# Three rotating score banks and one expert bank in the first layer of a two-layer attention kernel

## The chip, the cores and the metric

One Trainium2 chip, one core. The metric is device time in microseconds (us) of one execution; times are medians of several executions, and the profile is of one further execution.

## The reference

For 16 batches of 256 tokens of width 256 the reference applies two layers, each with an attention block and a feed-forward block. In layer 0 the feed-forward block holds a small attention across the 16 heads of each token, followed by eight dense experts weighted by a softmax gate:

```python
x = x + tanh(g_xattn[0]) * L0_xattn(layernorm(x), ctx, ctx, mask, causal)   # 16 heads of 64
x = x + tanh(g_ffn[0])   * L0_ffn(layernorm(x))
x = x + tanh(g_xattn[1]) * L1_xattn(layernorm(x), ctx, ctx)                 # 16 heads of 16
x = x + tanh(g_ffn[1])   * L1_ffn(layernorm(x))

# inside L0_ffn, b tokens, h2 the normalised middle result
att  = softmax(einsum('bthd,btgd->bthg', q, k) / sqrt(HD))      # heads against heads, per token
out  = einsum('bthg,btgd->bthd', att, v)
x    = x + (out @ Wo + bo)
gate = softmax(h2 @ Wg + bg)                                    # 8 experts
x    = x + einsum('btd,edf,bte->btf', h2, We, gate)
```

## The kernel before

Layer 0 runs to its end, writes its result to memory, and layer 1 then reads it. The change is in layer 0 alone.

Layer 0 is a software pipeline over batches. One body handles batch a's attention, batch b = a-1's heads-against-heads attention, and batch c = a-2's experts, and projects keys and values of the next batch ahead. Bodies 0 to 15 hold attention; bodies 2 to 15 hold all three; two more bodies (no attention, then experts alone) drain the pipeline. Each engine runs its own fixed program of the same 20 steps a body; engines meet only by semaphores, and within an engine everything is in order. So where an instruction waits, everything behind it on that engine waits too.

At step s of a body:

- **PE (TensorE)**: at even s, `pair_scores` of heads s and s+1; then the batch-b products of `mix_at`, then the expert of `expert_at` (`moe_experts`, 12 matmuls into one PSUM bank); then `head_transpose` of head s-3, at odd s `pair_values` of heads s-5 and s-4, then the projections of `own_at` and `ahead_at` (k1 of the next batch at step 11, v0 at 13, k2 at 16, v2 at 19). After step 19 comes `attn_out` (32 matmuls, L910). A body starts with the transposes of batch c's heads result (`oT`, L809), which wait for `gathered`.
- **DVE (VectorE)**: `attn_max` of head s (reads the score bank and frees it, L681), `attn_sum` of head s-1, then the batch-b and batch-c work: `moe_experts` at the steps of `add_at` (adds the gated expert into `acc`, two instructions, L665, and frees the bank), then x^T's low half at step 10 (L545), `mix_scores` at the steps of `score_at` (L591, a reduction of a product made by POOL), the softmax divide at step 13 (L608), and `mix_gather` at the steps of `gather_at` (L614).
- **POOL (GpSimd)**: four products of q and k (L321), then, when the divide is done, four products of weights and v (`weigh`, L335), each handed to one `mix_gather`.
- **ACT (ScalarE)**: exponentials, normalising, and the copies of projections and transposes out of PSUM.

Within a step DVE issues the expert's add before `mix_scores` and before `mix_gather`.

PSUM has eight banks here. `Banks` gives each use of a group of banks a turn: use k of a batch takes bank k mod count, the writer waits until `free` shows that the use before it in that bank was emptied, and the last reader raises `free`. Before, the groups were attention 2, score 2, heads 1, mix 1, moe 2. The moe group serves, in this order, `oT`, `out`, `h2T`, `gate` and the experts `we0` to `we7`. `gather_at`, `score_at` and `ahead_at` stay as they are:

```python
score_at = {7: 0, 9: 1, 11: 2, 12: 3}
gather_at = {15: 0, 16: 1, 18: 2, 19: 3}
```

Of the kernel before, what the change touches and what calls it, by code (L numbers as in the profile page):

```python
# [23 lines left out]
H = 16  # L24
# [6 lines left out]
E = 8  # L31
# [14 lines left out]
class Banks:  # L46
# [30 lines left out]
    def emptied(self, engine, use, batch):  # L77

        _, _, free, turn = self.at(use, batch)
        engine.wait_ge(free, turn + 1)  # L80

    def open(self, engine):
        for f in self.free:
            engine.sem_inc(f, 1)
# [7 lines left out]
def wait_apart(engine, passed, sem, value):  # L92

    engine.wait_ge(sem, value)
    engine.sem_inc(passed, 1)
# [20 lines left out]
def layer0(nc, ins, x2):  # L116
    with ExitStack() as ctx:
        def sb(name, shape, dtype=F32):
            return ctx.enter_context(nc.sbuf_tensor("l0_" + name, shape, dtype))
# [5 lines left out]
        def pair(name, shape):  # L125
            return sb(name + "_hi", shape, F32R), sb(name + "_lo", shape, F32R)
# [3 lines left out]
        wg, we = pair("wg", [P, ND, E]), pair("we", [P, ND, E * D])  # L130
# [19 lines left out]
        oT = qT  # L150
# [8 lines left out]
        glog, gmax, gsum, gate = sb("glog", [P, NT, E]), sb("gmax", [P, NT]), sb("gsum", [P, NT]), sb("gate", [P, NT, E])  # L159
        y, acc, h2T = sb("y", [P, NT, D]), sb("acc", [P, NT, D]), pair("h2T", [P, ND, S])  # L160
# [10 lines left out]
        attn = Banks(nc, ctx, "l0_attn", attn_uses + ["out"], ahead=["xT", "k0", "k1", "k2", "v0", "v2"])  # L171

        mix_at = {2: "hT", 3: "q", 4: "down", 5: "up0", 6: "up1"}
        expert_at = {6: 0, 7: 1, 8: 2, 10: 3, 12: 4, 14: 5, 15: 6, 17: 7}
        add_at = {7: 0, 8: 1, 9: 2, 10: 3, 12: 4, 14: 5, 15: 6, 17: 7}
        score_at = {7: 0, 9: 1, 11: 2, 12: 3}

        gather_at = {15: 0, 16: 1, 18: 2, 19: 3}
        score = Banks(nc, ctx, "l0_score", [f"s{j}" for j in range(H)])
        heads = Banks(nc, ctx, "l0_heads", [f"o{j}" for j in range(4)], 1)  # L180
        mix = Banks(nc, ctx, "l0_mix", ["hT", "q", "down", "up0", "up1"], 1)
        moe = Banks(nc, ctx, "l0_moe", ["oT", "out", "h2T", "gate"] + [f"we{j}" for j in range(E)])

        raw_in, split_hi, split_lo = [sem("raw_in0"), sem("raw_in1")], sem("split_hi"), sem("split_lo")
        mask_in, scored = sem("mask_in"), sem("scored")
# [34 lines left out]
        with nc.Block() as block:  # L220
# [579 lines left out]
            def _(pe):  # L800
                T = nc.tensor

                def transpose4(banks, use, batch, src):

                    ps, full, free, turn = banks.at(use, batch)
                    pe.wait_ge(free, turn)
                    for c in range(ND):
                        for t in range(NT):
                            last = T.transpose(ps[:, c * S + t * P:c * S + (t + 1) * P], src[:, t, c * P:(c + 1) * P], ident[:])  # L809
                    last.then_inc(full, 1)  # L810
# [19 lines left out]
                def tokens(banks, use, b, x, w, cols):  # L830

                    ps, full, free, turn = banks.at(use, b)
                    pe.wait_ge(free, turn)
                    for t in range(NT):
                        last = product3(nc, ps[:, t * cols:(t + 1) * cols],
                                        [(x[0][:, c, t * P:(t + 1) * P], x[1][:, c, t * P:(t + 1) * P], w[0][:, c, :], w[1][:, c, :])
                                         for c in range(ND)])
                    last.then_inc(full, 1)
# [29 lines left out]
                def pair_scores(a, j):  # L868

                    c = j // HPC  # L870
                    ps0, full0, free0, turn0 = score.at(f"s{j}", a)
                    ps1, full1, free1, turn1 = score.at(f"s{j + 1}", a)
                    pe.wait_ge(free0, turn0)
                    pe.wait_ge(free1, turn1)
                    T.matmul(ps0[:, 0:S], qT[rows0, c, P:S], kT[rows0, c, :], start=True, stop=True)  # L875
                    T.matmul(ps1[:, 0:S], qT[rows1, c, P:S], kT[rows1, c, :], start=True, stop=True)
                    T.matmul(ps0[:, S:CAUSAL], qT[rows0, c, 0:P], kT[rows0, c, 0:P], start=True, stop=True).then_inc(full0, 1)  # L877
                    T.matmul(ps1[:, S:CAUSAL], qT[rows1, c, 0:P], kT[rows1, c, 0:P], start=True, stop=True).then_inc(full1, 1)

                def head_transpose(a, j):  # L880

                    ps, full, free, turn = attn.at(f"T{j}", a)
                    pe.wait_ge(free, turn)
                    pe.wait_ge(norm_done, H * a + j + 1)
                    T.transpose(ps[:, 0:P], probs[:, j % 4, S:CAUSAL], ident[:])
                    T.transpose(ps[:, P:S], probs[:, j % 4, 0:P], ident[:])
                    T.transpose(ps[:, S:CAUSAL], probs[:, j % 4, P:S], ident[:]).then_inc(full, 1)  # L887
# [15 lines left out]
                def attn_out(a):  # L903
                    ps, full, free, turn = attn.at("out", a)
                    if first(a):
                        pe.wait_ge(wo_in, 16)
                    pe.wait_ge(free, turn)
                    for t in range(NT):
                        for c in range(NC0):
                            last = T.matmul(ps[:, t * D:(t + 1) * D], oT[:, c, t * P:(t + 1) * P], wo[:, c, :], start=c == 0, stop=c == NC0 - 1)  # L910
                    last.then_inc(full, 1)

                def project(use, a):

                    if use == "xT":
                        pe.wait_ge(xn_ready, a + 1)
                        transpose4(attn, "xT", a, xn)
                    elif use[0] == "q":
                        features(use, a, wq, xT)
                    elif use[0] == "k":  # L920
                        if use == "k0":
                            pe.wait_ge(ctx_ready, a + 1)
                        features(use, a, wk, cT)
                    else:
                        values(int(use[1:]), a)
# [25 lines left out]
                def body(a, b, c, nxt):  # L951
                    if c is not None:
                        pe.wait_ge(gathered, 4 * (c + 1))
                        transpose4(moe, "oT", c, o)
                    if a is not None:
                        attn.emptied(pe, "xT", a)
                        project("q0", a)
                        project("q1", a)
                    if c is not None:
                        moe.emptied(pe, "oT", c)  # L960
                        tokens(moe, "out", c, foT, fo, D)
                    if a is not None:
                        attn.emptied(pe, "v2", a)
                        attn.emptied(pe, "q0", a)
                    for s in range(STEPS):
                        if a is not None and s < H and s % 2 == 0:
                            if s % 4 == 0 and s > 0:
                                attn.emptied(pe, f"q{s // 4}", a)
                            if s == 12:
                                attn.emptied(pe, "k3", a)  # L970
                            pair_scores(a, s)
                        if a is not None and s == LAG_T:
                            head_transpose(a, 0)
                        beside_head(b, c, s)
                        if a is not None:
                            if LAG_T < s < H + LAG_T:
                                head_transpose(a, s - LAG_T)
                            if s >= LAG_V0 and s % 2 == 1:
                                if s - LAG_V0 == 8:
                                    for use in ("v1", "v3"):  # L980
                                        _, _, emptied, turn = attn.at(use, a)
                                        wait_apart(pe, pe_passed, emptied, turn + 1)
                                pair_values(a, s - LAG_V0)
                            if s in own_at:
                                project(own_at[s], a)
                        if nxt is not None and s in ahead_at:
                            project(ahead_at[s], nxt)
                    if a is not None:
                        heads.emptied(pe, "o2", a)
                        heads.emptied(pe, "o3", a)  # L990
                        attn_out(a)

                pe.wait_ge(consts, 1)
                for use in attn.ahead:
                    if use in ("k0", "v0"):
                        pe.wait_ge(split_lo, 1 + ("k0", "v0").index(use))
                    project(use, 0)
                pe.wait_ge(split_lo, NS_FIRST)
                body(0, None, None, 1)
                pe.wait_ge(split_lo, NS)  # L1000
                body(1, 0, None, 2)
# [712 lines left out]
```

## Time and profile before

| what | value |
|---|---|
| median of 3 runs | 2658.98 us (2656.93 to 2663.84) |
| the profiled execution, own time | 2655.57 us |
| its span, first to last instruction | 2653.8 us |
| PE busy, share of the span | 87% |
| DVE / ACT / POOL busy | 56% / 48% / 39% |
| mean granted TensorE clock | 0.958 |

The span is cut by engine and by line. A busy PE is not PE at its peak. In the timelines and waits, the part after an arrow names what ended an idle stretch: `[2.17 <-DVE l_negmax L681]` says that the engine sat idle for 2.17 us until DVE's instruction of line 681 was done. PEclk is the granted share of TensorE's full clock in a stretch.

### The profile page before, as it was taken

Reading aid. Unit: us, or ns where it says so; the run is one execution under the profiler, and the core shown is the slowest. Engines: PE = TensorE matmul, PEld = TensorE weight load, DVE = VectorE, ACT = ScalarE, POOL = GpSimd, SP = SyncE. Lnnn points to the kernel's source line nnn. Section 1 sums busy time; section 2 is a strip of 40 time slices with the busy share of each in tenths; the row PEclk is TensorE's granted clock in tenths of the full one; section 3 lists DMA queues with packets and bytes.
Section 4 is the critical chain, followed back from the end, with each engine's and each line's share of the span. In section 5 each row is a group of like instructions: output and inputs, shape, how many; then the busy total and the mean of one; then the engine's idle time right before and its main releaser. Section 6 shows DMA issues by size and latency. Waiting matters only on the chain. (4 is left out here: it accounts for less than half of the span.)

```text
span 2653.8 us, 48232 instructions
## 1 busy us (share of the span) xinstructions
PE 2302.0 (87%) x16128; PEld 1929.3 (73%) x16128; DVE 1493.3 (56%) x3906; ACT 1267.8 (48%) x3971; POOL 1022.9 (39%) x910
## 2 busy tenths in 40 slices
PE   5888888888888888888456999999999999999998
PEld 4667777777777777776344777877777887777777
DVE  3467667676766776767645445444444544444441
ACT  5655566555556555556023444433344443334441
POOL 1355564555554555555512333221233322123320
PEclk8999999999989999999677999999999999999999
DMA  4000000000000000000040000000000000000000
GB/s 145 14 6 17 13 16 4 16 16 16 16 12 4 16 16 16 16 4 9 4 161 1 13 17 16 16 16 16 4 12 16 16 16 16 16 4 12 16 9 9
DMA packets 25856, 51.66 MB, mean 19 GB/s; under 512 B 6272, under 2 KB 7040, under 8 KB 24640
## 3 DMA queue, kind: packets, MB, share of 16 engines
q1 hardware_dynamic: 25792, 50.84, 5.7%
q8 instruction: 37, 0.61, 0.1%
q14 instruction: 27, 0.22, 0.0%
HBM read 42.44 MB, written 8.39 MB: 19 GB/s over the span
## 5 line engine op out<-in xcount | busy, mean ns | idle before, releaser
L1157 POOL TENSOR_SCALAR l_probs<-l_probs,l_rinv 128x256 f32<-128x256 f32 x512 | 238.9, 482 | 587.0 <-DVE l_rinv L1372 585.3
L1268 ACT ACTIVATE l_probs<-l_score,l_negmax 128x256 f32<-128x256 f32 x512 | 238.9, 473 | 264.6 <-DVE l_negmax L1367 264.6
L335 POOL TENSOR_TENSOR l_prod<-l_att,l_kv 128x2048 f32<-128x2048 f32 x64 | 288.3, 4545 | 181.2 <-DVE l_att L608 181.2
L321 POOL TENSOR_TENSOR l_prod<-l_q,l_kv 128x2048 f32<-128x2048 f32 x64 | 290.3, 4548 | 151.7 <-DVE l_att L591 80.8
L1572 PE MATMUL l_ffn<-l_w,l_hid 128*128 128x256 f32 x1536 | 347.1, 381 | 1.0 <-ACT l_hid L1242 1.0
L1572 PEld LDWEIGHTS l_ffn<-l_w,l_hid 128*128 128x128 f32 x1536 | 287.0, 190 | 50.1 <-issue 13.5
L1379 DVE COPY l_probsT<-l_attn 128x512 f32<-128x512 f32 x256 | 175.4, 685 | 157.6 <-PE l_attn L1535 157.3
L681 DVE CUSTOM_DVE_ANT_0 l_probs<-l_score,l_mbias 128x256 f32<-128x256 f32 (+1 forms) x512 | 161.2, 352 | 140.2 <-PE l_score L877 91.8
L1367 DVE TENSOR_REDUCE l_negmax<-l_score 128x2 f32<-128x512 f32 x256 | 174.9, 683 | 64.4 <-PE l_score L1523 64.4
L614 DVE TENSOR_REDUCE l_h<-l_prod 128x128 f32<-128x2048 f32 x64 | 146.3, 2286 | 103.4 <-POOL l_prod L335 102.4
L427 ACT COPY l_probsT<-l_attn 128x384 f32<-128x384 f32 x256 | 121.1, 473 | 143.8 <-PE l_attn L887 143.8
L410 ACT ACTIVATE l_probs<-l_probs,l_negmax 128x256 f32<-128x256 f32 x256 | 130.9, 511 | 104.4 <-DVE l_negmax L681 104.4
L110 PE MATMUL l_moe<-l_we_hi,l_h2T_hi 128*128 128x256 f32 x512 | 160.1, 313 | 12.4 <-DVE l_acc L665 10.7
L1242 ACT ACTIVATE l_hid<-l_ffn,l_b 128x256 f32<-128x256 f32 x384 | 161.5, 478 | 11.9 <-PE l_ffn L112 10.1
L1535 PE MATMUL l_attn<-l_ident,l_probs 128*128 128x128 f32 x1024 | 154.9, 277 | 9.4 <-DVE l_probsT L1379 7.3
L875 PE MATMUL l_score<-l_kT,l_qT 64*128 64x256 f32 x256 | 98.2, 467 | 61.2 <-DVE l_negmax L681 61.2
L110 PE MATMUL l_attn<-l_cT_hi,l_wk_hi 128*128 128x256 f32 x384 | 122.8, 320 | 31.8 <-DVE l_xT_lo L545 31.8
L591 DVE TENSOR_REDUCE l_att<-l_prod 128x128 f32<-128x2048 f32 x64 | 145.9, 2279 | 5.8 <-issue 3.9
L111 PE MATMUL l_moe<-l_we_lo,l_h2T_hi 128*128 128x256 f32 x512 | 147.9, 289 | 0.0
L112 PE MATMUL l_moe<-l_we_hi,l_h2T_lo 128*128 128x256 f32 x512 | 147.7, 289 | 0.0
L1535 PEld LDWEIGHTS l_attn<-l_ident,l_probs 128*128 128x128 f32 x1024 | 118.7, 142 | 23.6 <-issue 10.0
L665 DVE SCALAR_TENSOR_TENSOR l_acc<-l_moe,l_gate,l_acc 128x256 f32<-128x256 f32 x256 | 110.7, 474 | 40.8 <-PE l_moe L112 26.7
(273 smaller groups left out, 7441.9 us busy)
## 6 DMA issues: line engine op xcount, KB each, us to landing
l_ctxin<-in_ctx SPq DMA_DIRECT2D x32, 256.0 KB, 3.0
l_xin<-in_x SPq DMA_DIRECT2D x16, 256.0 KB, 2.7
l_x<-in_x SPq DMA_DIRECT2D x16, 256.0 KB, 2.6
x<-l_acc SPq DMA_DIRECT2D x16, 256.0 KB, 2.0
l_xin<-x SPq DMA_DIRECT2D x16, 256.0 KB, 3.3
l_x<-x SPq DMA_DIRECT2D x16, 256.0 KB, 2.7
out<-l_x SPq DMA_DIRECT2D x16, 256.0 KB, 2.0
l_hid<-in_w SPq DMA_DIRECT2D x2, 1536.0 KB, 9.7
```

The lines of the kernel that those rows point to most:

```text
L110: last = nc.tensor.matmul(out, wh, xh, start=n == 0, stop=False)
L111: last = nc.tensor.matmul(out, wh, xl, start=False, stop=False)
L321: nc.gpsimd.tensor_tensor(prod[:, u].rearrange("p (h g d) -> p h g d", h=half, g=H), q4[:, u * half:(u + 1) * half].unsqueeze(2).to_broadc ...
L335: nc.gpsimd.tensor_tensor(prod[:, u].rearrange("p (h d g) -> p h d g", h=half, d=HD), a4.unsqueeze(2).to_broadcast([P, half, HD, H]), v4.u ...
L681: last = V.tensor_tensor_reduce(out=probs[:, j % 4, lo:hi], in0=ps[:, lo:hi], in1=mbias[:, lo:hi], scale=-HD0 ** -0.5, scalar=3e38, op0=AL ...
L1157: last = nc.gpsimd.tensor_scalar(probs[:, j % 4, t * S:(t + 1) * S], probs[:, j % 4, t * S:(t + 1) * S], rinv[:, j, t:t + 1], 1.0, ALU.mul ...
L1242: last = nc.scalar.activation(hid[:, c, :], ps[:, u * S:(u + 1) * S], ACT.Relu, bias=b1[:, c:c + 1])
L1268: last = nc.scalar.activation(probs[:, s % 4, t * S:(t + 1) * S], ps[:, t * S:(t + 1) * S], ACT.Exp, bias=negmax[:, s, t:t + 1], accum_out ...
L1367: V.tensor_reduce(negmax[:, j], ps[:].rearrange("p (t k) -> p t k", t=NT), axis=AX.X, op=ALU.max, negate=True).then_inc(max_ready, 1)
L1379: V.tensor_copy(probsT[:, j % 3, :], ps[:]).then_inc(free, 1)
L1535: last = T.transpose(ps[:, kt * S + t * P:kt * S + (t + 1) * P], probs[:, j % 4, t * S + kt * P:t * S + (kt + 1) * P], ident[:])
L1572: last = T.matmul(ps[:, 0:D], hid[:, c, t * P:(t + 1) * P], w2[:, c, :], start=c == 0, stop=c == 3 * NHC - 1)
```

## The change

The score group has three banks in place of two. A batch has 16 scores, which three banks do not divide, so two idle turns are added: PE itself passes them (`skip`) after step 19, ahead of the waits for `attn_out`. The moe group has one bank in place of two, and the steps at which PE computes an expert and at which DVE adds it are moved.

```diff
+    def skip(self, engine, use, batch):
+
+        _, full, free, turn = self.at(use, batch)
+        engine.wait_ge(free, turn)
+        engine.sem_inc(full, 1)
+        engine.sem_inc(free, 1)
...
-        expert_at = {6: 0, 7: 1, 8: 2, 10: 3, 12: 4, 14: 5, 15: 6, 17: 7}
-        add_at = {7: 0, 8: 1, 9: 2, 10: 3, 12: 4, 14: 5, 15: 6, 17: 7}
+        expert_at = {6: 0, 8: 1, 10: 2, 11: 3, 13: 4, 15: 5, 17: 6, 18: 7}
+        add_at = {7: 0, 8: 1, 10: 2, 12: 3, 14: 4, 16: 5, 17: 6, 19: 7}
...
-        score = Banks(nc, ctx, "l0_score", [f"s{j}" for j in range(H)])
+        score = Banks(nc, ctx, "l0_score", [f"s{j}" for j in range(H)] + ["idle0", "idle1"], 3)
...
-        moe = Banks(nc, ctx, "l0_moe", ["oT", "out", "h2T", "gate"] + [f"we{j}" for j in range(E)])
+        moe = Banks(nc, ctx, "l0_moe", ["oT", "out", "h2T", "gate"] + [f"we{j}" for j in range(E)], 1)
...
                     if a is not None:
+                        score.skip(pe, "idle0", a)
+                        score.skip(pe, "idle1", a)
+                    if a is not None:
                         heads.emptied(pe, "o2", a)
                         heads.emptied(pe, "o3", a)
                         attn_out(a)
```

## Rows read from the trace of the kernel before

**Rows 1.** Chain that ended last: its first piece (start us, us, what).
```profile
1359.86 6.97 DMA l_hid<-in_wk
```

**Rows 2.** Windows, one body: length; busy of PE, PEld, DVE, ACT, POOL; PEclk; DMA.
```profile
952.64:1031.06 78.42, 67.76 (x489) 57.21 (x489) 55.08 (x155) 45.38 (x142) 42.65 (x17) 0.98 0.04 14
```

**Rows 3.** Waits of PE in 910 to 990 us: total, times, longest.
```profile
PE l_score L875 <- DVE l_negmax L681: 3.8, 3, 2.2
PE l_attn L110 <- DVE l_xT_lo L545: 1.8, 1, 1.8
```

**Rows 4.** Timeline of PE in that body (start, us, line, operands, idle before).
```profile
966.62 0.36 PE L110 MATMUL l_mix<-l_fq_hi,l_hT_hi 128*128 128x256 f32 x1 [0.81 <-DVE l_hT_lo L549]
...
985.03 0.38 PE L110 MATMUL l_moe<-l_we_hi,l_h2T_hi 128*128 128x256 f32 x1
...
986.54 0.28 PE L885 MATMUL l_attn<-l_ident,l_probs 128*128 128x128 f32 x1
...
990.62 0.45 PE L875 MATMUL l_score<-l_kT,l_qT 64*128 64x256 f32 x1 [0.52 <-DVE l_negmax L681]
...
997.29 0.39 PE L110 MATMUL l_attn<-l_cT_hi,l_wk_hi 128*128 128x256 f32 x1 [1.82 <-DVE l_xT_lo L545]
...
1008.57 0.45 PE L875 MATMUL l_score<-l_kT,l_qT 64*128 64x256 f32 x1 [2.17 <-DVE l_negmax L681]
...
1017.12 0.28 PE L885 MATMUL l_attn<-l_ident,l_probs 128*128 128x128 f32 x1
...
1018.96 0.33 PE L885 MATMUL l_attn<-l_ident,l_probs 128*128 128x128 f32 x1 [0.55 <-ACT l_kT L402]
...
1022.46 7.07 PE L910 MATMUL l_attn<-l_wo,l_qT 128*128 128x256 f32 x32
1031.06 0.65 PE L809 MATMUL l_moe<-l_ident,l_h 128*128 128x128 f32 x4 [1.53 <-DVE l_h L614]
```

**Rows 5.** Timeline of DVE in that body.
```profile
979.07 0.42 DVE L681 CUSTOM_DVE_ANT_0 l_probs<-l_score,l_mbias 128x256 f32<-128x256 f32 x1 [3.38 <-PE l_score L877]
...
984.10 0.88 DVE L665 SCALAR_TENSOR_TENSOR l_acc<-l_moe,l_gate,l_acc 128x256 f32<-128x256 f32 x2 [1.00 <-ACT l_gate L462]
...
990.39 0.08 DVE L681 DVE_READ_ACCUMULATOR2_ANT l_negmax<- 128x1 f32 x1
...
996.54 0.69 DVE L545 TENSOR_TENSOR l_xT_lo<-l_attn,l_xT_hi 128x512 fp32r<-128x512 f32 x1 [1.36 <-ACT l_xT_hi L393]
...
1004.04 2.29 DVE L591 TENSOR_REDUCE l_att<-l_prod 128x128 f32<-128x2048 f32 x1 [0.16 <-issue]
...
1009.78 0.69 DVE L608 TENSOR_TENSOR l_att<-l_att,l_asum 128x512 f32<-128x512 f32 x1
...
1019.68 2.29 DVE L614 TENSOR_REDUCE l_h<-l_prod 128x128 f32<-128x2048 f32 x1 [2.15 <-POOL l_prod L335]
1021.88 0.87 DVE L665 SCALAR_TENSOR_TENSOR l_acc<-l_moe,l_gate,l_acc 128x256 f32<-128x256 f32 x2
```

**Rows 6.** Timeline of POOL in that body.
```profile
1010.55 18.04 POOL L335 TENSOR_TENSOR l_prod<-l_att,l_kv 128x2048 f32<-128x2048 f32 x4 [12.19 <-DVE l_att L608]
```

**Rows 7.** The page's costliest groups: DVE's read of a score bank.
```profile
L681 DVE CUSTOM_DVE_ANT_0 l_probs<-l_score,l_mbias 128x256 f32<-128x256 f32 (+1 forms) x512 | 161.2, 352 | 140.2 <-PE l_score L877 91.8
```

**Rows 8.** Windows over one projection each: q3, then k1 (seventh field PEclk).
```profile
976.35:977.96 1.61, 1.61 (x15) 1.48 (x13) 0.00 (x0) 1.61 (x9) 1.61 (x1) 1.00 0.00 0
997.29:999.95 2.66, 2.66 (x12) 2.44 (x12) 2.66 (x6) 1.75 (x7) 1.07 (x1) 0.55 0.00 0
```

**Rows 9.** Timeline of DVE in the last body (experts alone): first and last of eight adds.
```profile
1345.72 0.88 DVE L665 SCALAR_TENSOR_TENSOR l_acc<-l_moe,l_gate,l_acc 128x256 f32<-128x256 f32 x2 [1.50 <-PE l_moe L112]
...
1355.64 0.88 DVE L665 SCALAR_TENSOR_TENSOR l_acc<-l_moe,l_gate,l_acc 128x256 f32<-128x256 f32 x2 [0.54 <-PE l_moe L112]
```

**Rows 10.** Waits of PE for score banks in bodies 0 and 1 (35 to 95, 95 to 164 us).
```profile
PE l_score L875 <- DVE l_negmax L681: 1.8, 1, 1.8
...
PE l_score L875 <- DVE l_negmax L681: 2.7, 3, 1.7
```

## The prediction

> **What bounds the kernel now.** I read the chain of waits first: its first piece is a load of layer 1's weights at 1359.86 us [rows 1]. Nothing of layer 0 is overlapped with layer 1, so every microsecond by which layer 0's end moves goes into the total, and layer 1 stays as it is. Next the windows: one body of layer 0 lasts 78.42 us, of which PE is busy 67.76 at a granted clock of 0.98 [rows 2]. PE is the fullest engine, but 10.7 us a body are waits. The list of PE's waits has the one at which the change aims on top: 3.8 us, three times a body, for a score bank that DVE has not yet read [rows 3].
>
> Then the timeline, to see which wait ends last. Bodies begin with the oT transposes, at 952.64 and 1031.06 here. The second waited 1.53 us for DVE's last gather (L614) [rows 4]. That gather hangs on POOL: four products take 18.04 us and start when DVE's softmax divide (L608) is done, at 1009.78 + 0.69 = 1010.47 [rows 5, 6]. So a body is 57.8 us from oT to the divide, and 20.6 from the divide over POOL to the next oT. PE, with all its score waits, is done 1.53 us before that. Score waits at the batch's end are therefore already paid for by POOL; what counts is when the divide is done, and whether PE's own path behind it stays under 20.6 us.
>
> **What the change gives.** With three banks a pair of scores needs the bank reads of two and three heads back, not of the last one. I replay the body in order.
>
> Up to 966.62 nothing is gained. The pair of heads 2 and 3 loses its wait (3.8 - 0.52 - 2.17 = 1.1 us [rows 3, 4]), but 4 us later PE waits again, 0.81, for hT's low half [rows 4], which follows ACT's and DVE's work on heads 0 and 1; both engines are full there, so the 1.1 is added to the 0.81. From 966.62 to the expert of step 6 PE's order is unchanged.
>
> Step 7 and 8: expert 1 now stands behind the scores of step 8. It needs DVE's add of expert 0, done at 984.10 + 0.88 = 984.98 [rows 5]. That add waits for ACT's gate, which doesn't move. So PE stands until 985.03, where expert 2 started before [rows 4]: from there both kernels run alike, the new one with one expert less done.
>
> Step 9 and 10: DVE has no add in step 9, so its reduction `mix_scores` 1 starts at 990.5, right behind the head read that ends at 990.47 [rows 5]. The pair of step 10 loses its 0.52 wait. DVE then does 2.29 (a reduction, as the row at 1004.04), two head reads of 352 ns and add 2 (0.88): done at 994.3 [rows 5, 7]. Expert 3, now at step 11, waits for this add: 994.3 + 0.15 (a bank freed at 990.47 was used at 990.62 [rows 4, 5]) = 994.45. It takes 1.5 us (985.03 to 986.54 [rows 4]), the transposes and pair values behind it 1.3 (1018.96 - 0.55 - 1017.12 [rows 4]), so k1 starts at 997.2, as before (997.29). It no longer waits for x^T: the low half was written at 996.54 + 0.69 [rows 5], behind ACT's work on head 10, and head 10 is read some 0.9 earlier now.
>
> k1 took 2.66 us at a granted clock of 0.55, near the lower level of 1.2 GHz, where q3, the same 12 matmuls, took 1.61 at 1.00, or 2.4 GHz [rows 8]. The fall came behind the 1.82 us wait. I take 1.61, since the longest wait ahead of it is now about 1.1 us (expert 3), and keep 2.66 for the range. Scores of step 12 then start at 998.8 instead of 999.95, at full clock. DVE reads a head 1.1 after its pair began at full clock (979.07 for the pair that followed q3 at 977.96 [rows 5, 8]), then adds expert 3, which has long been computed, and reaches the last `mix_scores` at 998.8 + 1.1 + 0.7 + 0.9 = 1001.5, against 1004.04 [rows 5]. Call this gain g: 2.5 us. Its bounds: with k1 at the low clock 1.2; if DVE never waited for scores of step 12, 3.2. The divide, and with it POOL, comes g earlier.
>
> **What it takes.** With one bank expert j cannot start before add j-1, and PE stands at an expert with all behind it. Expert 5 (step 15) waits for add 4, behind the divide; expert 6 for add 5, behind gather 0; expert 7 (step 18) for add 6, and DVE has add 6 in step 17, behind gather 1 of step 16. Gather 1 waits for POOL's second product: 1019.68, and the add behind it ends at 1021.88 + 0.87 = 1022.75 [rows 5]. Before, no PE instruction waited for that add; PE started `attn_out` at 1022.46 [rows 4]. Now expert 7 starts at 1022.75 + 0.15 - g = 1022.9 - g, takes 1.5, and behind it stand the transposes of head 15, the last pair values and v2: 3.5 us (1018.96 to 1022.46 [rows 4]). `attn_out` starts at 1027.9 - g, 5.4 - g later than before. Its length is unchanged (7.07). 1.53 of the 5.4 was idle time before oT, so the body grows by 5.4 - 1.53 - g = 3.9 - g: 1.4 us with g = 2.5, between 0.7 and 2.7. From the divide to oT it is now 24.4 us, PE's path, no longer POOL's 20.6. The gain of 2.5 is real, but more than used up.
>
> A second cost is the clock. New waits of 1 to 3 us stand ahead of experts 3 to 7. A fall of the clock behind expert 5 or 6 is covered, as PE waits again soon after. Behind expert 7 nothing covers it: one projection at the low clock costs 1.05 [rows 8]. I count half of it, 0.5 a body; the bounds are 0 and 1.3 (1.05 for the expert, 0.25 for the transposes by the same ratio).
>
> `skip` adds two waits for banks that were freed several steps earlier, and four increments, to PE's queue; no row prices it. Its bounds are 0 and one handover (0.15) a body; I take 0, nearest to a wait that is already met.
>
> The last body holds experts alone: eight adds from 1345.72 to 1355.64, one in 1.42 us [rows 9]. With one bank expert and add alternate: 1.5 + 0.88 + 2 x 0.15 = 2.7, seven times 1.3 more, 9 us. At the low clock (1.05 more per expert) it is 16. PE now works half the time there; I take 11. The body before it stays: its adds are spread between reductions and it waits for POOL. Bodies 0 and 1 have no experts, only score waits, 1.8 and 2.7 [rows 10]; I take 2 saved, between 0 and 4.5.
>
> The Trainium skill says, in Perfetto Trace Analysis, section Matmuls, that independent matmul groups should rotate through PSUM banks so that reading one out overlaps the next group's matmuls. By that rule every expert after the first would stand for its add, about 2765 us in all. The rows put other PE work between most experts and their adds, and the sum here charges only the waits left over.
>
> **Sum.** Fourteen bodies with experts: 14 x (1.4 + 0.5) = 27. Last body 11, first two -2. Together +36 on the profiled execution's own 2655.6 gives 2691. That execution is 3.4 below the median of the three runs, 0.1%, so I predict 2691 for the median too: 1.2% slower.
>
> **The rivals.**
> *Clock falls on the path (slower still).* k1 stays at the low clock (g = 1.2) and expert 7 runs low too: 14 x (2.7 + 1.3) + 16, with nothing saved in the first two bodies, = +72, 2728 us. For it: k1 has a low clock now behind a wait of 1.8 [rows 3, 8], and the new body has more waits. Against it: a wait of 2.17 at 1008.57 was followed by scores of 0.45 us, full speed [rows 4]. The Trainium skill, in TensorE: Matmul & The Clock Gate, section on depth-cycling of the PSUM queue, tells of a kernel whose short idles between bank turns made the clock go up and down; the 0.98 of the body [rows 2] shows only one such fall now.
>
> *The waits only move (same).* If g reached 3.7 to 3.9, the body would keep its length: +0 to 3 for the bodies, +9 for the last, -4 for the first two: about 2662. It needs DVE nearly without a wait from step 10 to 12, while scores of step 12 still stand behind k1.
>
> *The score waits were the bound (faster).* If PE finds add 6 done when it comes to expert 7, POOL's chain stays the bound and g = 2.5 is kept: 14 x -2.5 + 9 - 2 = -28, 2628 us. Place: expert 7 at step 18. It decides from 5.4 us: so much earlier add 6 would have to be, ahead of gather 1 rather than behind it; DVE's order says no.
>
> *Each expert pays its add.* Seven experts a body stand for the whole add and its handover, 0.88 + 0.15 [rows 3 to 5]: 14 x 7 x 1.03 + 9 = +110, 2765 us. Against it: only experts 3 to 7 come to an add that is late, and expert 1 found DVE where expert 2 did.
>
> **Chances and range.** Forecast (2670 to 2706) 0.57; clock rival 0.22; same 0.10; faster 0.09; every add paid 0.02. The forecast's own range: g = 3.2 and no clock loss, 14 x 0.7 + 9 - 4.5 = +14, 2670; and half the clock loss more, 2706. The range 2658 to 2728 leaves out the faster rival and the last. Within 0.3% (8 us, about what a measurement of this kernel can tell) 0.10, faster 0.09, slower 0.81.
>
> **What would show it.** Right: PE's wait list has score waits under 1 us a body and a new entry, experts (L110 of moe) waiting for L665, of 5 us or more a body, longest at steps 15 and 18; oT waits no more for L614; POOL's four products start about 2.5 us earlier after oT; the last body is 9 to 16 longer. Wrong: bodies under 78.4 us, or oT still waiting for L614, which would mean that expert 7 isn't on the path; or k1 still at the low clock, which would make it slower.

## The result, and the profile after

The changed kernel takes 2703.97 us (median of 4 runs, 2696.82 to 2709.58), the kernel before on the same chip 2658.2. The ratio is 1.0167, with a 95% interval of 1.0138 to 1.0195. The profiled execution is the slowest of the four, 2709.58 us with a span of 2707.8.

The chain of waits again has a load of layer 1's weights as its first piece (start, us, what):

```profile
1407.72 4.77 DMA l_hid<-in_wk
```

It started at 1359.86 before [rows 1], so layer 0 is 47.9 us longer in this execution. Layer 1, whose code is the same, took 2707.8 - 1407.72 = 1300.1 against 2653.8 - 1359.86 = 1293.9. The runs below give from 1294.5 to 1300.1 for it, so these 6 us are differences between executions.

Windows over two whole bodies, and over three stretches inside the second (length; busy of PE, PEld, DVE, ACT, POOL; PEclk; DMA share; GB/s):

```profile
565.02:644.37 79.35, 68.61 (x489) 56.73 (x488) 54.57 (x154) 45.64 (x142) 42.09 (x18) 0.98 0.04 14
482.31:565.02 82.71, 72.80 (x489) 60.73 (x488) 54.58 (x154) 45.74 (x142) 42.89 (x18) 0.92 0.04 13
504.30:507.70 3.40, 3.40 (x19) 3.20 (x17) 2.02 (x9) 1.88 (x7) 0.45 (x1) 0.52 0.00 0
514.90:518.30 3.40, 3.40 (x21) 3.08 (x21) 0.00 (x0) 2.04 (x9) 3.40 (x2) 0.57 0.00 0
548.60:555.80 7.20, 6.63 (x32) 5.59 (x33) 3.53 (x9) 3.36 (x13) 7.20 (x2) 0.53 0.00 0
```

One body was 78.42 before [rows 2]. Two bodies of the same work now differ by 3.4 us. PE is busy 4.2 us longer in the slow one: it runs the same 489 matmuls, and in the three stretches the granted clock is near 0.5. (Bodies are counted here from one `attn_out` to the next.)

The list of PE's waits in 910 to 990 us (total, times, longest):

```profile
PE l_moe L117 <- DVE l_acc L672: 7.4, 6, 2.6
PE l_heads L905 <- ACT l_probsT L434: 1.1, 3, 0.7
PE l_mix L117 <- DVE l_hT_lo L556: 1.1, 1, 1.1
```

The score waits of [rows 3] are gone, and so is the one for x^T. In their place stand experts that wait for an add. The timeline of PE in the body at full clock shows where (start, us, line, operands, idle before):

```profile
565.02 7.07 PE L917 MATMUL l_attn<-l_wo,l_qT 128*128 128x256 f32 x32
...
585.87 0.36 PE L117 MATMUL l_mix<-l_fq_hi,l_hT_hi 128*128 128x256 f32 x1 [1.11 <-DVE l_hT_lo L556]
...
604.35 0.38 PE L117 MATMUL l_moe<-l_we_hi,l_h2T_hi 128*128 128x256 f32 x1 [1.23 <-DVE l_acc L672]
...
620.61 0.39 PE L117 MATMUL l_moe<-l_we_hi,l_h2T_hi 128*128 128x256 f32 x1 [1.26 <-DVE l_acc L672]
...
628.94 0.38 PE L117 MATMUL l_moe<-l_we_hi,l_h2T_hi 128*128 128x256 f32 x1 [2.62 <-DVE l_acc L672]
...
639.41 0.39 PE L117 MATMUL l_moe<-l_we_hi,l_h2T_hi 128*128 128x256 f32 x1 [1.28 <-DVE l_acc L672]
...
644.37 7.07 PE L917 MATMUL l_attn<-l_wo,l_qT 128*128 128x256 f32 x32
651.27 0.60 PE L816 MATMUL l_moe<-l_ident,l_h 128*128 128x128 f32 x4
```

These are experts 1, 4, 5 and 7. The oT transposes at the end wait for nothing; before, they waited 1.53 for DVE's last gather [rows 4]. DVE in the same body and in the last one, and POOL in the same body:

```profile
626.46 0.69 DVE L615 TENSOR_TENSOR l_att<-l_att,l_asum 128x512 f32<-128x512 f32 x1
...
636.29 2.29 DVE L621 TENSOR_REDUCE l_h<-l_prod 128x128 f32<-128x2048 f32 x1 [1.01 <-POOL l_prod L342]
638.49 0.86 DVE L672 SCALAR_TENSOR_TENSOR l_acc<-l_moe,l_gate,l_acc 128x256 f32<-128x256 f32 x2
...
1385.02 0.88 DVE L672 SCALAR_TENSOR_TENSOR l_acc<-l_moe,l_gate,l_acc 128x256 f32<-128x256 f32 x2 [1.92 <-PE l_moe L119]
...
1403.51 0.88 DVE L672 SCALAR_TENSOR_TENSOR l_acc<-l_moe,l_gate,l_acc 128x256 f32<-128x256 f32 x2 [1.76 <-PE l_moe L119]
```

```profile
627.23 18.02 POOL L342 TENSOR_TENSOR l_prod<-l_att,l_kv 128x2048 f32<-128x2048 f32 x4 [10.47 <-DVE l_att L615]
```

The divide ends at 627.15, which is 41.28 us after the token mix began at 585.87 (in both kernels some 14 us behind the start of oT); before it was 1010.47 - 966.62 = 43.85 [rows 4, 5]. So the divide did come 2.57 us earlier. Expert 7 starts at 639.41, right behind add 6 (638.49 + 0.86 = 639.35), and that add stands behind gather 1.

The two rows of DVE at 1385 and 1403 us are the first and the last of the eight adds of the last body: 18.5 us from one to the other, against 9.9 before [rows 9].

**Where the 47.9 us are.** `attn_out` of body 1 starts 1.2 later than before; the 13 bodies after it last 81.15 on average against 78.65, together +32.5; body 15 takes 80.3 against 73.3, +7.0; what follows the last `attn_out` takes 114.4 against 107.3, +7.1. The sum is 47.8.

**The clock, body by body.** I read the granted clock of all bodies in windows of 1 us. In the changed kernel it falls at three places, counted from a body's start: about 21 us (behind the wait ahead of the token mix), 30 us (behind the gate of step 5) and 65 us (around expert 5 and its wait). From 240 us on the bodies sort by that: 79.35 with a short fall at 65 alone, 80.9 with one at 30 and a short one at 65, 81.2 with one at 30 and a long one at 65, 82.4 to 82.7 with one at 21 as well. So a fall at 21 or 30 costs about 1.55, a short one at 65 nothing and a long one 0.3, since PE waits soon after for the adds of experts 6 and 7. There are 13 such early falls in the 13 bodies.

### The profile page after: what moved, and what is told of

It reads as the page before. It is cut to its first block and busy times, and to the rows that moved or that the text cites. A ratio compares the mean times of both kernels' runs of the same rounds, so it can differ in the third digit from the quotient of the medians.

```text
span 2707.8 us, 48308 instructions
## 1 busy us (share of the span) xinstructions
PE 2344.8 (87%) x16128; PEld 1949.4 (72%) x16128; DVE 1486.7 (55%) x3906; ACT 1272.0 (47%) x3971; POOL 1019.9 (38%) x910
## 5 line engine op out<-in xcount | busy, mean ns | idle before, releaser
L117 PE MATMUL l_moe<-l_we_hi,l_h2T_hi 128*128 128x256 f32 x512 | 167.0, 326 | 127.8 <-DVE l_acc L672 127.1
L117 PEld LDWEIGHTS l_moe<-l_we_hi,l_h2T_hi 128*128 128x128 f32 x512 | 104.9, 205 | 157.5 <-DVE l_acc L672 149.6
L1252 ACT ACTIVATE l_hid<-l_ffn,l_b 128x256 f32<-128x256 f32 x384 | 161.0, 476 | 11.9 <-PE l_ffn L119 10.1
L1152 POOL TENSOR_TENSOR l_rstdF<-l_varF,l_neghalf 128x2 f32<-128x2 f32 x16 | 11.2, 701 | 318.6 <-DVE l_varF L1314 318.6
```

The lines of the kernel that those rows point to most:

```text
L117: last = nc.tensor.matmul(out, wh, xh, start=n == 0, stop=False)
```

## The experiments

Twelve kernels ran, in three groups of four, each group on one chip beside the kernel before (2657.3 to 2658.7 us).

**First group: which part costs?** The kernel before with the moved steps alone (two banks each, as before):

```diff
-        expert_at = {6: 0, 7: 1, 8: 2, 10: 3, 12: 4, 14: 5, 15: 6, 17: 7}
-        add_at = {7: 0, 8: 1, 9: 2, 10: 3, 12: 4, 14: 5, 15: 6, 17: 7}
+        expert_at = {6: 0, 8: 1, 10: 2, 11: 3, 13: 4, 15: 5, 17: 6, 18: 7}
+        add_at = {7: 0, 8: 1, 10: 2, 12: 3, 14: 4, 16: 5, 17: 6, 19: 7}
```

> The kernel before with only the two step tables of the change (expert_at, add_at); score banks 2, moe banks 2. My theory: the gain g of 2.5 us a body comes from the moved adds (DVE reaches the divide earlier), not from the third score bank; with two moe banks expert 7 needs only add 5, so POOL's chain stays the bound and a body takes 78.4 - 2.5 = 75.9 us: 14 x -2.5 = -35, about 2623 us (2612 to 2640). Rival A, the third score bank brings the gain: without it nothing is gained, about 2658.

Measured: 2627.25 us, ratio 0.9887 (0.9867 to 0.9907). Two bodies in its windows:

```profile
770.80:846.40 75.60, 66.22 (x490) 55.83 (x489) 54.85 (x154) 45.08 (x142) 42.67 (x18) 1.00 0.05 14
846.40:922.00 75.60, 66.18 (x490) 55.80 (x489) 54.86 (x154) 45.06 (x142) 42.70 (x18) 1.00 0.05 14
```

The whole gain lies in the moved steps, and it needs no bank: bodies are 2.8 us shorter than 78.42, though PE still waits 54.6 us for score banks between 164 and 1180 us. This version beats both kernels. (In the kernel before the waits for score banks are 49.3 us in the same stretch.) It moved the steps of the experts and those of the adds together, so which of the two tables brings the gain, no run separates.

The changed kernel with two score banks and no idle turns:

```diff
-        score = Banks(nc, ctx, "l0_score", [f"s{j}" for j in range(H)] + ["idle0", "idle1"], 3)
+        score = Banks(nc, ctx, "l0_score", [f"s{j}" for j in range(H)])
...
-                        score.skip(pe, "idle0", a)
-                        score.skip(pe, "idle1", a)
```

> The changed kernel with the score banks put back to two (no idle turns); moe 1 bank and the new step tables stay, one PSUM bank lies idle. My theory: score waits return (about 3 us a body in PE's wait list) but stand where PE has time over, so a body keeps its 79.4 us at full clock and the time is 2680 to 2705; it is nearer 2680 if the wait of step 2, now back, keeps the clock from falling in steps 3 to 5. Rival A, the third score bank brings the gain g: 2.5 us a body slower than the changed kernel, about 2739.

Measured: 2701.08 us, ratio 1.0165 (1.0144 to 1.0186), the time of the changed kernel. Its list of PE's waits, 164 to 1180 us, has the score waits back:

```profile
PE l_moe L117 <- DVE l_acc L672: 78.4, 74, 2.4
PE l_score L882 <- DVE l_negmax L688: 24.3, 38, 1.1
```

They cost nothing here: the two intervals overlap almost wholly, so beside one expert bank the third score bank earns nothing. What costs is the single expert bank: 2701 against 2627 with the same steps.

The changed kernel with adds 5 to 7 one step earlier (15, 16, 18 in place of 16, 17, 19), with three score banks and then with two:

```diff
-        add_at = {7: 0, 8: 1, 10: 2, 12: 3, 14: 4, 16: 5, 17: 6, 19: 7}
+        add_at = {7: 0, 8: 1, 10: 2, 12: 3, 14: 4, 15: 5, 16: 6, 18: 7}
```

> The changed kernel with adds 5, 6 and 7 on DVE one step earlier each (steps 15, 16, 18), so that adds 5 and 6 stand ahead of gathers 0 and 1. My theory, expert 7 behind gather 1 is the path: its wait goes, attn_out starts some 2.7 us earlier after oT, a body takes 76.7 us at full clock; with the 1.7 us that the low clock costs now 78.4: 2640 to 2670, 1.3 to 2.4% faster than the changed kernel. Rival B, expert 7's wait isn't on the path (the loss is the low clock alone): 2700, no change.

> As the run with the earlier adds, but with two score banks. My theory: the third score bank is worth little, so it is within 0.5% of that run, 2640 to 2680. Rival A: 2.5 us a body slower than that run, 35 us.

Measured: 2698.96 us (ratio 1.0154, 1.0118 to 1.0189), and 2667.65 (ratio 1.0034, 1.0009 to 1.0058; 7 runs from 2651.57 to 2684.96). The first missed its expectation. The second lies in its range of times, but it is 1.2% faster than the first, where at most 0.5% had been expected. In the first one's trace the waits of experts 6 and 7 are gone, as meant. But these waits had covered the fall behind expert 5, which now counts: in the version with two score banks a body with that fall alone lasts 78.6, one with none 76.0. Windows over a body and its slow stretch, and from PE's timeline the expert in whose wait that stretch begins:

```profile
480.40:560.60 80.20, 70.87 (x489) 59.00 (x488) 54.79 (x155) 45.76 (x142) 43.39 (x18) 0.94 0.04 13
544.60:551.20 6.60, 5.42 (x25) 4.39 (x26) 4.14 (x15) 2.69 (x9) 6.60 (x2) 0.53 0.00 0
```

```profile
545.77 0.58 PE L117 MATMUL l_moe<-l_we_hi,l_h2T_hi 128*128 128x256 f32 x1 [2.62 <-DVE l_acc L672]
```

The version with two score banks has falls in most bodies too, but two bodies without any, which shows what the order of work alone takes:

```profile
397.50:473.50 76.00, 66.35 (x489) 55.93 (x488) 53.81 (x155) 45.30 (x142) 40.54 (x18) 1.00 0.04 14
552.60:632.80 80.20, 70.59 (x489) 59.52 (x488) 55.16 (x155) 45.51 (x142) 43.32 (x18) 0.94 0.04 13
```

Here the third score bank costs 31 us, clear of the noise. With it the wait ahead of the token mix is 1.1 us, with two banks 0.8, and falls at 21 us stand only in versions with three: in 8 of the 13 bodies of this one, in 3 of the changed kernel, in none of any version with two. That the longer wait brings them is likely, but two versions below have three banks, the same wait and none of these falls in their 13 bodies.

Thus the clock became the theory to test.

**Second group: steps, and the clock.** The changed kernel with the old tables of steps:

```diff
-        expert_at = {6: 0, 8: 1, 10: 2, 11: 3, 13: 4, 15: 5, 17: 6, 18: 7}
-        add_at = {7: 0, 8: 1, 10: 2, 12: 3, 14: 4, 16: 5, 17: 6, 19: 7}
+        expert_at = {6: 0, 7: 1, 8: 2, 10: 3, 12: 4, 14: 5, 15: 6, 17: 7}
+        add_at = {7: 0, 8: 1, 9: 2, 10: 3, 12: 4, 14: 5, 15: 6, 17: 7}
```

> The changed kernel (three score banks, one expert bank) with the old tables of steps for experts and adds. Question: are the moved steps, taken with one bank, what costs, or what saves? Theory (an expert with one bank pays for an add that comes right before it in time): expert 1 now follows expert 0 by one step and stands for add 0, which waits for the gate on ACT; experts 2, 3, 6 and 7 follow their adds closely too. Some 4 to 5 us a body more than in the changed kernel, 14 x 4.5 = 63: 2750 to 2780 us, and the list of PE's waits has the wait of experts for the adds at twice its share or more. Rival (one bank is free of cost where the steps are old, because the adds are done as early as they can be): 2660 to 2700 us.

Measured: 2770.13 us, ratio 1.0423 (1.0405 to 1.044). One body, and PE's wait at expert 1:

```profile
584.90:670.20 85.30, 71.10 (x489) 58.95 (x488) 54.97 (x154) 45.55 (x142) 42.35 (x18) 0.94 0.04 13
```

```profile
625.47 0.58 PE L117 MATMUL l_moe<-l_we_hi,l_h2T_hi 128*128 128x256 f32 x1 [3.52 <-DVE l_acc L672]
```

The time is as expected. The waits for adds rose only from 85.9 to 95.3 us between 164 and 1180 us, not to twice as much. In the 13 full bodies (1109.2 us against 1055.0) PE stands idle 45.5 us longer and is busy 8.8 longer. So most of the loss is waiting: besides the adds, PE waits again for x^T (16.3 us in that stretch) and for the last gather (11.9, against 1.5 in the changed kernel). The clock, which falls at expert 1 in every full body and at 59 us in nearly all, has the smaller part. With the old steps the two changes of banks together cost 112 us; the moved steps bring 66 back in this setting and 30 in that of the kernel before.

Adds 4 to 7 one step earlier, so that no add that an expert waits for stands behind the divide:

```diff
-        add_at = {7: 0, 8: 1, 10: 2, 12: 3, 14: 4, 16: 5, 17: 6, 19: 7}
+        add_at = {7: 0, 8: 1, 10: 2, 12: 3, 13: 4, 15: 5, 16: 6, 18: 7}
```

> The changed kernel with adds 4 to 7 one step earlier each (13, 15, 16, 18), so that no expert stands for an add behind the divide or behind gather 1. Theory: what the change costs at full clock is the wait of experts 5 to 7, and the falls of the clock come behind expert 5's wait of 2.6 us. With add 4 ahead of the divide that wait is gone, the divide is 0.87 later than in the changed kernel and still 1.7 earlier than in the kernel before, bodies are about 76.7 us, and the time is 2635 to 2655 us. No stretch of low clock starts behind expert 5. Rival (some wait always makes the clock fall, wherever it stands): the falls only move to another wait, and the time stays at 2680 to 2700 us.

Measured: 2664.6 us, ratio 1.0024 (1.0014 to 1.0035). Windows over two bodies and over the slow stretch of the second:

```profile
392.80:469.40 76.60, 67.10 (x490) 55.58 (x489) 54.48 (x154) 45.41 (x142) 42.44 (x18) 1.00 0.04 14
...
625.70:703.80 78.10, 68.56 (x490) 56.87 (x489) 54.47 (x154) 45.53 (x142) 42.49 (x18) 0.98 0.04 14
656.70:660.20 3.50, 3.50 (x22) 2.94 (x18) 0.00 (x0) 2.46 (x11) 3.50 (x1) 0.55 0.00 0
```

The body at full clock is what the theory said, and no stretch starts at expert 5 any more (62 us into a body); two of 13 bodies have one at 68 us, behind a wait of 1.5 for ACT's probabilities. But the fall at 30 us comes in 11 of 13 bodies, so the time ends 10 us above the theory's range. The rival (falls only move) is refuted for the place behind expert 5, not for the one at 30 us.

Extra matmuls ahead of PE's waits, in the version with one expert bank and two score banks (2701.08), and ahead of expert 5 alone in the version that took 2667.65 (the first has two more calls of `fill`, ahead of the query tokens and of the scores of step 2):

```diff
+                def fill(n):
+                    for _ in range(n):
+                        T.matmul(spare[:, 0:P], ident[:], ident[:], start=True, stop=True)
...
+                            if b is not None and expert_at[s] in fills:
+                                fill(fills[expert_at[s]])
                             moe_experts(c, expert_at[s])
```

> One expert bank, two score banks without the idle turns, the steps of the changed kernel, and in PE's waits extra matmuls of the identity with itself into a PSUM bank of its own, whose results nobody reads (9 ahead of expert 1, 6 of expert 3, 9 of expert 4, 20 of expert 5, 9 of expert 7, 6 ahead of the query tokens, 8 ahead of the scores of step 2). Its partner without the extra matmuls took 2701. Theory (the falls of the clock come from PE standing still, and cost 1.6 us a body): the clock stays up through the body, bodies come to 79.4 us, the time to 2675 to 2685 us and the clock of the span to 0.965 or more. Rival (the clock falls for another reason, such as the power of the work itself, or the extra matmuls delay what they stand ahead of): 2700 us or more.

> The version with adds 5 to 7 one step earlier and two score banks, which took 2667.65, with 20 extra matmuls of the identity with itself (results unread) ahead of expert 5 alone, where PE stood for 2.6 us. Theory (the idle time ahead of expert 5 makes the clock fall behind it): no stretch of low clock starts behind expert 5, bodies come to 76.0 us, which that version had where the clock held, and the time to 2630 to 2645 us. Rival (the fall has another cause, or moves to the wait ahead of another expert): 2660 to 2680 us.

Measured: 2743.39 us (ratio 1.0314, 1.0294 to 1.0335) and 2689.71 (1.0116, 1.0099 to 1.0133). Both missed, and PE's timeline of the second shows one reason. Before it stands the wait that was to be filled, from the version without the extra matmuls:

```profile
461.39 0.39 PE L117 MATMUL l_moe<-l_we_hi,l_h2T_hi 128*128 128x256 f32 x1 [2.37 <-DVE l_acc L672]
...
622.89 4.63 PE L938 MATMUL l_spare<-l_ident 128*128 128x128 f32 x40
```

A call makes two matmuls, 0.23 us together, so 20 calls lasted 4.6 us where PE had waited 2.4 (the 2.6 of the expectation is the wait with three score banks): the filling pushed the experts back; in the first kernel the bodies at full clock are 82.8 for that reason, in the second the one body without a fall takes 77.9 in place of 76.0. The second has also a fall at 30 us in 12 of 13 bodies, which average 80.0; that is as much again. Of the clock both already say what the theory said: in the bodies up to 1200 us no fall is left at expert 5.

**Third group: the same with fillings about as long as the waits, and two questions left.**

> As the version with extra matmuls ahead of expert 5 alone, with half as many (10 calls, which the trace of that run shows as 20 matmuls, 2.3 us, against a wait of 2.6): 20 calls lasted 4.6 us and pushed expert 5 back. Theory (the idle time ahead of expert 5 brings the fall behind it, and nothing else was wrong there): no low clock between 61 and 69 us into a body, bodies of 76.0 us, or 77.6 where the clock falls at 30 us, and 2635 to 2655 us; the partner without extra matmuls took 2667.65. Rival (so short a filling does not hold the clock): falls behind expert 5 as before, 2660 to 2675 us.

Measured: 2644.07 us, ratio 0.9948 (0.9932 to 0.9965), 23.6 less than without the extra matmuls. The filling ahead of expert 5, and windows over two bodies:

```profile
371.85 2.40 PE L938 MATMUL l_spare<-l_ident 128*128 128x128 f32 x20
...
310.50:386.50 76.00, 68.61 (x510) 58.28 (x509) 55.18 (x155) 45.26 (x142) 42.71 (x18) 1.00 0.05 14
386.50:464.00 77.50, 70.12 (x509) 59.59 (x508) 55.10 (x155) 45.38 (x142) 42.64 (x18) 0.98 0.04 14
```

No fall at expert 5 is left in the 13 bodies, where the version without the filling has one in 11; bodies are 76.0, or 77.5 with a fall at 30 us. Expert 5 starts when it did, and a body without a fall is as long as before, so it is the clock that gained. Work that nobody needs made the kernel faster.

> As the version with extra matmuls in all of PE's waits, with about half as many (5, 3, 5, 10, 5 ahead of experts 1, 3, 4, 5, 7; 3 ahead of the query tokens; 4 ahead of the scores of step 2), since the first filling lasted longer than the waits. The order of experts and adds is that of the changed kernel, with two score banks; without extra matmuls it took 2701. Theory (of the changed kernel's 81.15 us a body some 1.7 are falls of the clock): falls at 21 and 65 us into a body vanish, the one at 30 us stays in about half of the bodies as it did with the first filling, bodies are 79.4 and 81 us by turns, and the time is 2680 to 2695 us. Rival (what the falls cost is hidden, and the bodies keep 81 us without them): 2698 to 2710 us.

Measured: 2691.66 us, ratio 1.0125 (1.0108 to 1.0141), against 1.0165 without the filling. Its windows:

```profile
401.80:481.20 79.40, 74.52 (x559) 64.27 (x558) 54.96 (x154) 45.36 (x142) 42.66 (x18) 1.00 0.04 14
481.20:562.20 81.00, 76.14 (x559) 65.62 (x559) 54.95 (x154) 45.49 (x142) 42.69 (x18) 0.98 0.04 13
```

The order of experts and adds alone, at full clock, gives 79.4 us. The falls at 21 and 65 us are gone from the 13 bodies up to 1202 us, and the one at 30 us is left in 6 of them. The theory is not shown by that. The version without the filling, with two score banks as well, has no fall at 21 either, one at 30 in 7 bodies and one at 65 in 12, and its bodies with a short fall at 65 alone take 79.3: the filling removed what PE's later waits had hidden. In the two profiled executions (2697.2 and 2697.0 us) layer 0 is equally long, 1400.3 and 1399.8 us. What the 9 us between the medians are stays open.

Adds 4 to 7 earlier with two score banks, and the same with fillings around the gate of step 5:

```diff
+                            if use == "up0":
+                                fill(2)
                             mix_up(b, int(use[2:]))
...
+                            fill(1)
                             moe_product("gate", c, wg, E)
+                            fill(2)
```

> The version with adds 4 to 7 one step earlier, which took 2664.6, with two score banks in place of three and no idle turns. Question: does the third bank earn anything once the experts no longer stand for late adds? Theory (no: its waits lie where DVE or the adds decide): 2655 to 2675 us, within 0.5% of 2664.6, with 20 us or more of score waits back. Rival (the third bank was held back only by the experts, and now pays): 2685 us or more.

> Adds 4 to 7 one step earlier, two score banks, and extra matmuls of the identity with itself (results unread) around the gate of step 5: 2 calls ahead of the token mix's up projection, 1 ahead of the gate's 12 matmuls of 8 columns and 2 behind them, some 1.1 us in all, of which 0.7 fill waits. Theory (the fall of the clock at 30 us into a body comes behind the two short waits and the narrow matmuls of the gate, not behind a long wait): the falls at 30 us vanish from most bodies, which come to about 77 us, and the time to 2645 to 2658 us. Rival (they have another cause): the falls stay and the time is 2664 to 2675 us.

Measured: 2657.67 us (ratio 0.9995, 0.9985 to 1.0004) and 2662.4 (1.0016, 1.0005 to 1.0027; 10 runs from 2654.38 to 2668.82). The first has 24.6 us of score waits back and says again that the third score bank earns nothing: 2657.67 with two, 2664.6 with three, and the intervals, each against the kernel before beside it, do not meet, so two banks are a little faster. The second is inconclusive: the fall at 30 us comes in 6 of 13 bodies against 9 of 13 without the filling, and most bodies without it take 77.1 to 77.4 instead of 76.6. What sets it off stays open.

## Why the prediction held, point by point

**The mechanism was right.** Score waits gone, the divide earlier, expert 7 behind add 6 behind gather 1, oT no longer waiting for the last gather: each is in the rows of after. Theory and rivals were told apart by the moved steps alone (2627, the gain without the bank) and by one expert bank with two score banks (2701, the loss without the third bank). The number is in part luck: the body at full clock was taken too dear and the clock too cheap, and the errors, 25 us one way and 13 the other, partly cancel. Nor does the upper end of the forecast's own range, 2706, follow from its words: half of the clock loss more is 14 x 0.5 = 7, which gives 2698. By that sum the measured 2704 lies above the forecast's own range, and only inside the wider one up to 2728.

**The gain g**: 2.57 us measured, 2.5 worked out. One clause was wrong: I put it down to both the third bank and the moved steps. The same tables with two banks in each group give bodies of 75.6, so the moved steps did it.

**The body at full clock**: +1.4 worked out, +0.93 to +1.0 measured (79.35 and 79.4 against 78.42). From the divide's end to `attn_out` I had 17.4 us, and it took 644.37 - 627.15 = 17.2. `skip`, taken as 0, costs hardly anything: bodies with a short fall at 65 alone last 79.3 to 79.5 with it, and 79.2 to 79.3 in the version with two score banks, which has none.

**The clock**, the step that was mis-sized: "0.5 a body, behind expert 7". No fall starts behind expert 7 in the bodies read. They start at 21 and 30 us, early in the body, where nothing covers them, and 13 of them at 1.55 make 20 of the 23 us by which the 13 bodies exceed 79.35 each; 7 had been counted. The statement beside it, that a fall behind expert 5 or 6 is covered, held, and its other half too: taking the covering waits away made it count. The rows were there to read: in the kernel before two of the bodies have such a fall. Its windows:

```profile
705.10:786.60 81.50, 72.31 (x490) 60.91 (x489) 55.18 (x154) 45.31 (x142) 42.60 (x18) 0.92 0.04 13
786.60:865.60 79.00, 69.21 (x489) 58.24 (x488) 54.74 (x154) 45.51 (x142) 41.69 (x18) 0.96 0.04 14
734.10:741.00 6.90, 6.90 (x37) 5.64 (x38) 1.23 (x8) 3.41 (x15) 5.93 (x2) 0.54 0.00 0
```

I had read one body and taken it for all. k1 is back at full clock, as said: the changed kernel shows no fall between 36 and 60 us in the 13 bodies.

**The last body**: 11 taken, 9 as the bound at full clock; the adds spread by 8.6 and the stretch grew by 7.1. They stand 2.64 apart, where 2.7 was worked out.

**Body 15** was counted like the others, +1.9, and grew by 7.0. Windows over it, after and before:

```profile
1212.96:1293.29 80.33, 65.51 (x438) 54.37 (x436) 51.81 (x146) 42.99 (x137) 40.65 (x15) 0.89 0.03 9
...
1179.31:1252.57 73.26, 60.22 (x437) 50.99 (x436) 51.88 (x147) 42.72 (x137) 40.04 (x15) 0.95 0.03 8
```

PE is busy 5.3 us longer with the same work, as the clock is low for 17 of the 80 us against 7 of 73, and idle 1.8 longer. It projects nothing for a next batch there, so less work stands between an expert and the add before it: its waits for adds are 10.6 us, 4.1 at expert 5, against 7.4 in the list above.

**The first two bodies**: -2 taken, +1.2 measured. The 1.2 lies ahead of PE's first matmul, which starts at 15.91 in place of 14.65. The two bodies keep their length: in body 0 PE waited 1.80 for a score bank and then 0.83 for ACT's probabilities, and now 3.33 for the probabilities. The score waits were covered by waits behind them.

**The sum**: predicted +36 for layer 0, +47.9 in this execution, the slowest of its kernel; the medians of the whole kernels differ by 45.8. Above the forecast: the clock's 1.8 in place of 0.5 a body (13 x 1.3 = 17), body 15 (5) and the first two (3). Below it: the body at full clock (13 x 0.47 = 6), the last one (4), and that the kernel before averages 78.65 a body and not 78.42 (13 x 0.23 = 3). 36 + 25 - 13 = 48.

**The rivals.** "The score waits were the bound" is refuted by the two score banks. "The waits only move" needed g near 3.8. "Clock falls on the path" put 2.6 us a body on k1 and expert 7; the falls that counted cost 1.8 and stood at the token mix and the gate. "Each expert pays its add" is near the waits for adds, 7.2 us a body against 7.4 in the list above, but not near the time: those waits stand for the most part in place of waits that the body had before, and the body at full clock grew by 1. The Trainium skill, in TensorE: Matmul & The Clock Gate, section on depth-cycling of the PSUM queue, tells of a kernel whose short idles between bank turns made the clock go up and down; the run with the filled wait ahead of expert 5 agrees, 2644 against 2668; filling the short waits around the gate did not help, 2662 against 2658. Its advice in Perfetto Trace Analysis, section Matmuls, to rotate independent groups through banks, agrees for the experts (two banks 2627, one 2701) and not for the scores, which rotate through two already: a third bank earned nothing.

## What to carry to other kernels

A bank in rotation is worth what its wait costs at the place that ends last: the longest entry of the wait list was free here, and the bank taken from the experts was not. (A third score bank beside two expert banks was not run.) Before adding buffers, try the order of the steps alone; it gave all of the gain. And read the granted clock over every repetition of a loop, not one: a wait that is "covered" can be what hides the slow stretch behind another.

## What the hardware showed that was not expected

A wait of 2.4 us ahead of expert 5 was enough for the granted clock to go to about 0.5 of full speed in or behind it, in 11 of 13 bodies of the same order; with 20 unused matmuls in the wait the fall was gone from all 13, and the whole kernel was 23.6 us (0.9%) faster. Behind the wait of 1.1 us ahead of the token mix such a fall comes in some bodies only (3 of 13 in the changed kernel); that this wait causes it was not tested by itself. In the 13 bodies of the changed kernel the low stretches last from 3.4 to 6.9 us. The fall at 30 us starts behind two waits of 0.40 and 0.27 us and twelve matmuls of 8 columns (1.3 us); in one kernel after another it comes in some bodies and not in others, and filling the short waits did not remove it. Why it comes in one body and not in the next stays open.
